# Working out the recurrence's gates in two halves: inside the first stage and inside attention

## The reference

```python
ig = (x @ Wi + bi).transpose(0, 2, 1)[..., None]      # x = [q, k, v]
fg = (x @ Wf + bf).transpose(0, 2, 1)[..., None]
log_f = jax.nn.log_sigmoid(fg)
log_f_cum = ... jnp.cumsum(log_f, axis=2)
log_D = tril(log_f_cum - log_f_cum^T) + ig^T
D = jnp.exp(log_D - max(log_D))
C = (qh @ kh^T) / sqrt(dh) * D
h = C / (max(|C.sum|, exp(-max_log_D)) + EPS) @ vh
```

## Time and profile before

| | us |
|---|---|
| median of 3 runs | 794.55 (789.97 to 797.62) |
| profiled execution | 790.37 |
| its span | 788.6 |
| first stages | 0 to 75.1 |
| gates' stage with its two ends | 75.1 to 104.5 |
| attention | 104.5 to about 314.5 |
| mixture | to 788.6 |

### The profile page before, as it was taken

How to read it: one execution, slowest core, us unless ns; L and a number is a source line. 1 busy time by engine, 2 the same in 40 slices (tenths; PEclk the granted TensorE clock), 3 DMA queues, 4 the chain that set the end, 5 groups by cost and what they waited for, 6 DMA issues and landing times.

```text
span 788.6 us, 20116 instructions
## 1 busy us (share of the span) xinstructions
PE 685.6 (87%) x7407; PEld 597.4 (76%) x7408; DVE 506.3 (64%) x992; ACT 409.3 (52%) x848; POOL 391.4 (50%) x594
## 2 busy tenths in 40 slices
PE   0785069999999886789999999999999999999994
PEld 0553057777777765678889998999999999999993
DVE  4762846777777787966338787533557666676750
ACT  0766246676666665544454232223556666666662
POOL 2111347888878875632111534132246675757654
PEclk9999579999999999999999999999999999999998
DMA  7982363544545721286761313243678787988854
GB/s 247 297 293 69 138 208 110 182 136 152 157 140 181 236 83 54 84 306 240 265 206 54 108 54 107 55 98 105 190 225 225 233 234 244 232 258 219 254 142 57
DMA packets 90726, 135.66 MB, mean 172 GB/s; under 512 B 16720, under 2 KB 44112, under 8 KB 90672
## 3 DMA queue, kind: packets, MB, share of 16 engines
q1 hardware_dynamic: 74128, 107.41, 41.7%
q0 software_dynamic: 7168, 17.04, 11.0%
q10 hardware_dynamic: 9376, 10.49, 4.2%
HBM read 92.32 MB, written 34.21 MB: 160 GB/s over the span
## 4 chain that ended last, share of the span: by engine, by line
PE 65%; DVE 7%; ACT 5%; DMA 4%; issue 2%; POOL 2%; SPq 0%; POOLq 0%; ACTq 0%; DVEq 0%
PE psH L1229 30%; PE psY L1249 15%; PE psO L702 4%; PE psQ L660 4%; PE ring L645 3%; PE ring L670 2%; ACT dec L744 2%; PE ring L676 2%; PE psT L1209 2%; DMA xT<-over13l 1%; DMA out<-ystage,sidx 1%; ACT state L757 1%; DMA amr<-am 1%; PE psR L1276 1%; DVE xl L1478 1%
## 5 line engine op out<-in xcount | busy, mean ns | idle before, releaser
L1229 PE MATMUL psH<-xh,w13h 128*128 128x256 f32 (+1 forms) x768 | 220.5, 287 | 2.8 <-issue 2.8
L1229 PE MATMUL psH<-xh,w13l 128*128 128x256 f32 (+1 forms) x768 | 215.2, 280 | 0.0
L1229 PE MATMUL psH<-xl,w13h 128*128 128x256 f32 (+1 forms) x768 | 214.9, 280 | 0.0
L1721 POOL TENSOR_TENSOR hl<-sg,hh 128x256 fp32r<-128x256 f32 (+1 forms) x96 | 79.4, 833 | 178.2 <-ACT hh L1352 177.7
L1229 PEld LDWEIGHTS psH<-xh,w13h 128*128 128x128 f32 (+1 forms) x768 | 137.8, 179 | 10.9 <-issue 10.0
L1229 PEld LDWEIGHTS psH<-xl,w13h 128*128 128x128 f32 (+1 forms) x768 | 138.0, 180 | 0.8
L1229 PEld LDWEIGHTS psH<-xh,w13l 128*128 128x128 f32 (+1 forms) x768 | 137.8, 179 | 0.0
L1347 ACT ACTIVATE sg<-psH 128x256 f32<-128x256 f32 (+1 forms) x96 | 36.4, 379 | 126.5 <-PE psH L1229 125.8
L1484 DVE TENSOR_TENSOR sg<-sg,psH 128x256 f32<-128x256 f32 (+1 forms) x96 | 39.9, 416 | 94.2 <-ACT sg L1347 94.2
L744 ACT ACTIVATE dec<-ring 128x512 f32<-128x512 f32 x128 | 74.0, 592 | 26.9 <-PE ring L648 26.2
L821 DVE SCALAR_TENSOR_TENSOR dec<-psQ,dec 128x512 f32<-128x512 f32 x128 | 79.3, 680 | 6.9 <-PE psQ L660 6.2
(11 more groups left out here) (224 smaller groups left out, 1397.5 us busy)
## 6 DMA issues: line engine op xcount, KB each, us to landing
raw<-w13T SPq DMA_DIRECT2D x64, 352.0 KB, 4.4
gcT<-ctxT ACTq DMA_DIRECT2D x8, 1024.0 KB, 5.8
kT<-ctxT SPq DMA_DIRECT2D x16, 512.0 KB, 5.6
ctxs<-ctx SPq DMA_DIRECT2D x16, 512.0 KB, 3.7
xn<-xnorm SPq DMA_DIRECT2D x16, 512.0 KB, 4.0
out<-xres SPq DMA_DIRECT2D x16, 512.0 KB, 4.8
raw<-w2T SPq DMA_DIRECT2D x16, 512.0 KB
qst<-qT_all SPq DMA_DIRECT2D x14, 512.0 KB, 6.4
```

The costliest lines, as they stand in the source:

```text
L1229: last = nc.tensor.matmul(psH[m][0:n, v, :], w[wp][:, c, col:col + n], x[xp][:, c, :], start=(c == 0 and k == 0), stop=(c == DC - 1 and k ...
L1721: nc.gpsimd.tensor_tensor(hs[u.p][1][0:n, m, :], sg[0:n, m, :], hs[u.p][0][0:n, m, :].bitcast(F32), ALU.subtract).then_inc(hl_ready, 1)
```

## The change

`gate_stage` is gone. What it did stands in four generators, one for each engine (`gates_vector`, `gates_scalar`, `gates_tensor`, `gates_saved` for SP), each working on one half of 256 columns; the code around it calls `next(gates)` where a piece shall run. Half 0 runs in the first stage (now `front_stage`), half 1 in attention.

- In the first stage the loops are written out. The gate rows of batches 0 to 7 are stored straight to `half.head` in SBUF, those of 8 to 15 to DRAM as before. VectorE does bias and absolute value ahead of measuring pair 7, `log1p_exp` between the norms of pairs 6 and 7, the rest behind. For pair 7 VectorE, not ScalarE, copies the queries from PSUM, in its `drain`. ScalarE does Exp and Ln at the end of step 5, the three exponentials and part 0 ahead of `keep(7)`, parts 1 and 2 behind; the subtractions are VectorE's. GpSimd builds the masks in steps 2 and 3. SP loads batch 0's keys and context between `store(5)` and `store(6)`; `store(7)` stands between the saves of part 1 and part 2; when all is saved it loads tile 0's decay rows, then the masks of the second buffers in three DMAs.
- The buffers of half 0 lie where `aml[1]` and `amr[1]` lie, those of half 1 on the first two batches of `qT_all` (the queries of batches 2 and 3).
- In attention tiles 0 to 14 are written out, then a loop of 3 x 4. VectorE has a piece at the end of tiles 6 (bias, absolute value), 7 (`log1p_exp`), 8 (F, am), 9 (M, -M, m), 10 (first subtraction), 11 (first `tmE` copy) and inside the take in tiles 11 (second subtraction), 12 and 13 (`tmE` copies). ScalarE has Exp and Ln in tile 7, three exponentials and part 0 in tile 10, parts 1 and 2 in tiles 11 and 12. TensorE has one transpose ahead of `back` in tiles 11, 12 and 13, all three into the same columns of `psO`. SP loads `head` in batch 3 and saves in batch 6; batch 8's decay load waits for the saves.
- The table load at attention's start is gone; tanh and the load of the exponentials' table are in step 3 of the first stage.

The diff, cut to its core (the removed stage is the one quoted above):

```diff
-                    sp.wait_ge(kept, 2 * p + k + 1)
+                    b = 2 * p + k
+                    sp.wait_ge(kept, b + 1)
                     for w in range(2):
-                        sp.dma_start(d.gt[w, bass.ds(2 * p + k, 1)].rearrange("b h t -> (b h) t"),
-                                     gst[k][w * NH:(w + 1) * NH, :]).then_inc(stored[k], 16)
+                        to = half.head[b * NH:(b + 1) * NH, w, :] if b < HB else d.gt[w, b]
+                        sp.dma_start(to, gst[k][w * NH:(w + 1) * NH, :]).then_inc(stored[k], 16)
...
-            for p in range(PAIRS - 4, PAIRS):
+            for p in range(4):
+                refill(p + 2, p % 2)
                 store(p)
+            for p in (4, 5):
+                store(p)
+            sp.dma_start(g.kT0[:, :, :], d.ctxT[0].rearrange("(c p) t -> p c t", p=P)).then_inc(g.kT_in[0], 16)
+            sp.dma_start(g.ctx0[:, :, :], d.ctx[0].rearrange("(c p) d -> p c d", p=P)).then_inc(g.ctx_in[0], 16)
+            store(6)
+            for n, _ in enumerate(gates_saved(sp, gt, half, 0, d)):
+                if n == 1:
+                    store(7)
+            sp.wait_ge(gt.saved, 16 * 4)
+            sp.wait_ge(gt.ex_turned, 3)
+            load_decay(sp, g, d, 0, 0, masks=(masks_ready, 2))
+            for rows, lo, hi in ((g.aml, 0, 3), (g.aml, 6, P), (g.amr, 3, P)):
+                sp.dma_start(rows[1][lo:hi, :, :], rows[0][lo:hi, :, :]).then_inc(g.masks_kept, 16)
             for k in range(2):
...
-            run(dve, step, lambda i, r: None, ch, 2 * 3)
+            gates = gates_vector(nc, g, gt, half, 0, ch, ((stored[0], 32 * 4), (stored[1], 32 * 4)), turned_to)
+            def step(p):
+                if p + 1 < PAIRS:
+                    if p + 1 == PAIRS - 1:
+                        next(gates)
+                    measure(p + 1)
+                norm(p)
+                if p == PAIRS - 2:
+                    next(gates)
+            def drain(p):
+                next(gates)
+                next(gates)
+                for k in range(2):
+                    n = 2 * p + k
+                    dve.wait_ge(xt_ready, n + 1)
+                    nc.vector.tensor_copy(g.qT_all[:, (n - 2) * DC:(n - 1) * DC, :], psT[k][:, :, :])
+                dve.wait_ge(tanh_ready, 1)
+                nc.vector.tensor_scalar(g.coef[:, :], g.coef[:, :], g.tanh[:, 0:1], None, ALU.mult)
+                for _ in gates:
+                    pass
+            measure(0)
+            run(step, drain)
         @block.gpsimd
         def _(pool):
...
+            gates = gates_scalar(nc, act, gt, half, 0)
...
+                if p == 3:
+                    act.wait_ge(later_in, 16 * LATER)
+                    nc.scalar.activation(g.tanh[:, :], g.branch[:, :], ACT.Tanh).then_inc(tanh_ready, 1)
+                    nc.scalar.preload_act_table_set("natural_log_exp_and_others")
+                if p == 5:
+                    next(gates)
+            def drain(p):
+                next(gates)
+                keep(p)
+                for _ in gates:
+                    pass
+            run(step, drain)
...
+def gates_vector(nc, g, gt, h, k, c, arrived, turned_to):
+    dve = c.eng
+    nc.vector.memset(h.ones, 1.0)
+    for sem, count in arrived:
+        dve.wait_ge(sem, count)
+    c.link(nc.vector.tensor_scalar(h.f, h.head[:, 1, :], g.bias[:, 1:2], None, ALU.add))
+    nc.vector.scalar_tensor_tensor(out=h.poly, in0=h.f, scalar=-1.0, in1=h.f, op0=ALU.mult,
+                                   op1=ALU.max).then_inc(gt.abs_ready, 1)
+    yield
+    dve.wait_ge(gt.e_ready, 2 * k + 1)
+    log1p_exp(nc, c, h.e, h.lu, h.poly, h.mask, (gt.e_ready, 2 * k + 2))
+    yield
+    c.link(nc.vector.scalar_tensor_tensor(out=h.f, in0=h.f, scalar=0.0, in1=h.lu, op0=ALU.min, op1=ALU.subtract))
+    c.link(nc.vector.tensor_tensor_scan(h.F, h.ones, h.f, 0.0, ALU.mult, ALU.add))
+    c.link(nc.vector.scalar_tensor_tensor(out=h.am[:, 0, :], in0=h.head[:, 0, :], scalar=g.bias[:, 0:1],
+                                          in1=h.F, op0=ALU.add, op1=ALU.subtract))
+    yield
+    c.link(nc.vector.tensor_tensor_scan(h.M, h.am[:, 0, :], h.am[:, 0, :], -3.0e38, ALU.max, ALU.max))
+    nc.vector.tensor_scalar(h.am[:, 1, :], h.M, -1.0, None, ALU.mult)
+    nc.vector.tensor_tensor(h.m, h.F, h.M, ALU.add).then_inc(gt.exps_go, 1)
+    yield
+    for q in range(2):
+        dve.wait_ge(gt.part_made, 3 * k + q + 1)
+        nc.vector.tensor_tensor(h.rest, (h.am, h.rest)[q], h.parts[q], ALU.subtract).then_inc(gt.rest_ready, 1)
+        yield
+    for n in range(3):
+        dve.wait_ge(gt.ex_turned, 3 * k + n + 1)
+        nc.vector.tensor_copy(g.tmE[:, n, k * P:(k + 1) * P], turned_to[n]).then_inc(gt.tm_taken, 1)
+        yield
+def gates_scalar(nc, act, gt, h, k):
+    act.wait_ge(gt.abs_ready, k + 1)
+    nc.scalar.activation(h.e, h.poly, ACT.Exp, scale=-1.0).then_inc(gt.e_ready, 1)
+    act.wait_ge(gt.e_ready, 2 * k + 1)
+    nc.scalar.activation(h.lu, h.e, ACT.Ln, bias=1.0).then_inc(gt.e_ready, 1)
+    yield
+    act.wait_ge(gt.exps_go, k + 1)
+    nc.scalar.activation(h.ex[:, 0, :], h.am[:, 0, 0:P], ACT.Exp, bias=h.am[:, 1, P - 1:P])
+    nc.scalar.activation(h.ex[:, 1, :], h.am[:, 1, P:S], ACT.Exp, bias=h.M[:, P - 1:P])
+    nc.scalar.activation(h.ex[:, 2:4, :].rearrange("p a t -> p (a t)"), h.m, ACT.Exp, scale=-1.0).then_inc(gt.exps, 1)
+    nc.scalar.activation(h.parts[0], h.am, ACT.Copy).then_inc(gt.part_made, 1)
+    yield
+    for q in range(1, 3):
+        act.wait_ge(gt.rest_ready, 2 * k + q)
+        nc.scalar.activation(h.parts[q], h.rest, ACT.Copy).then_inc(gt.part_made, 1)
+        yield
+def gates_tensor(nc, g, pe, gt, h, k, turned_to):
+    pe.wait_ge(gt.exps, k + 1)
+    for n, q in enumerate((0, 2, 3)):
+        if n > 0 and turned_to[n] is turned_to[n - 1]:
+            pe.wait_ge(gt.tm_taken, 3 * k + n)
+        nc.tensor.transpose(turned_to[n], h.ex[:, q, :], g.ident[:, :]).then_inc(gt.ex_turned, 1)
+        yield
+def gates_saved(sp, gt, h, k, d):
+    rows = slice(k * P, (k + 1) * P)
+    sp.wait_ge(gt.exps, k + 1)
+    sp.dma_start(d.em.rearrange("b h t -> (b h) t")[rows], h.ex[:, 1, :]).then_inc(gt.saved, 16)
+    for q in range(3):
+        sp.wait_ge(gt.part_made, 3 * k + q + 1)
+        sp.dma_start(d.am[:, q].rearrange("w b h t -> (b h) w t")[rows], h.parts[q]).then_inc(gt.saved, 16)
+        yield
+def load_decay(sp, g, d, b, c, masks):
+    sp.wait_ge(*masks)
+    sp.dma_start(g.aml[c][3:6, :, :], d.am[0][:, bass.ds(b, 1), :, c * P:(c + 1) * P].rearrange(
+        "q b h t -> q (b h) t")).then_inc(g.am_in[c], 16)
+    sp.dma_start(g.amr[c][0:3, :, :], d.am[1][:, bass.ds(b, 1), :, c * P:(c + 1) * P].rearrange(
+        "q b h t -> q (b h) t")).then_inc(g.am_in[c], 16)
...
-        R0, RPL, LOOPS = 3, 4, 6
+        R0, RPL, LOOPS = 15, 4, 3
...
+        GATES_ACT, GATES_DVE = (14, 20, 22, 24), (13, 15, 17, 19, 21, 23)
+        GATES_PE = (10, 11, 12)
+        turned_to = [psO[:, 0, 264:264 + P]] * 3
...
+                if b == HB:
+                    sp.wait_ge(gt.saved, 16 * 8)
+                load_decay(sp, g, d, b, 0, masks)
                 sp.wait_ge(qsc_ready, b)
                 load_em(b)
...
+                if b == 3:
+                    for u in range(2):
+                        sp.wait_ge(q_in[u], 16 * 2)
+                    sp.dma_start(half.head, d.gt.rearrange("w b h t -> (b h) w t")[P:2 * P]).then_inc(gt.head_in, 16)
                 sp.wait_ge(filled, decays_done(2 * b - 1))
-                load_decay(b, 1)
+                load_decay(sp, g, d, b, 1, masks)
+                if b == 6:
+                    for _ in gates_saved(sp, gt, half, 1, d):
+                        pass
                 if b == B - 3:
                     sp.wait_ge(q_in[0], 16 * (B // 2 - 2))
...
+                    next(gates)
                 for gg in range(4):
...
+                if r < R0 and 2 * r in GATES_ACT:
+                    next(gates)
...
-            nc.scalar.preload_act_table_set("natural_log_exp_and_others")
+            gates = gates_scalar(nc, act, gt, half, 1)
...
+                if r in GATES_PE:
+                    next(gates)
...
             def step(i, r, is_last):
                 for k in range(4):
                     weigh(i, r, k, decay_use(i, r, k))
+                if r < R0 and 2 * r in GATES_DVE:
+                    next(gates)
                 if r >= 1:
                     take(i, r - 1)
                 if r >= 2:
                     residual(i, r - 2)
+                if r < R0 and 2 * r + 1 in GATES_DVE:
+                    next(gates)
+            gates = gates_vector(nc, g, gt, half, 1, c_, ((gt.head_in, 16),), turned_to)
...
+                        pool.wait_ge(gt.tm_taken, 6)
                     keys(i, r + 1)
                     lift_values(i, r + 1, 0)
```

## The result

The changed kernel takes 803.06 us (median of 4 runs, 801.68 to 807.0) where the kernel before, on the same chip, takes 796.09 (4 runs): a ratio of 1.013, 95% interval 1.0092 to 1.0169. The forecast was 781.4. The profiled execution took 801.95, its span 799.9 where that of before is 788.6: 11.3 us longer.

The account below looks back on a forecast made before the run. A 29.4 us hole ahead of attention was taken as the bound: span 788.6 - 20.1 (front) + 7.0 (attention) = 775.5; against the median, 794.55 - 13.1 = 781.4 us, range 773 to 790.

Parts of the forecast that it names:

- The hole can be taken out: The 29.4 us gates' stage ahead of attention: what is taken from it comes off the end, unless attention gives it back.
- The store's wait: First stage, before measuring pair 7: VectorE waits for a 2.5 us gate-row store, shifting the rest by 1.5 us, bounds 0 and 4.
- The first decay at 83.5: Start of attention: the first decay matmul comes at 83.5 where it was 104.59, a gain of 21.1 us.
- The barrier falls under that load: Between first stage and attention: the block's barrier is hidden under tile 0's 2.3 us decay load.
- Tile 1's masks: Attention's tile 1: decay rows behind the mask copies, landing 2.5 to 5.6 us after issue, stall it 0 to 2.2, taken +1.0.
- The clock: Attention's start: TensorE again idles about 6 us beforehand, so nothing is given back for the slow first tile.
- Attention: Gates' work moved into attention's tiles costs +7.0 us: 5.0 of work, 2.0 of VectorE-GpSimd collisions; bounds 4 and 17.
- collisions dear: Rival: VectorE-GpSimd port collisions make attention cost +12 to +17 us, giving 786.5 to 791.5; chance 0.15.
- SP in batch 6: SP stands until tile 12 for part 2; tile 14's keys and decay load behind it aren't due earlier, costing nothing.
- The signs: Wrong if the first decay is after 90, or attention up to tile 14 loses under 3 or over 12 us.
- same: Outcome within one per cent of the median: half the poor-front and dear-collision rivals plus the hole that stays; chance 0.16.
- slower: Outcome slower than before: a rival at 805, twenty VectorE operations each behind a whole GpSimd one, had 0.04; outcome's chance 0.05.

Follow-up runs that it names:

- e3: The changed kernel with VectorE's bias and absolute value behind pair 6's norm, log1p behind pair 7's, ScalarE's Exp and Ln in step 6; 798.7 us, ratio 1.0067.
- e5: e11 with the mask copies issued behind the block's barrier and TensorE's wait for the weights moved to the first back; 782.71 us, ratio 0.9873.
- e11: The changed kernel with the edits of e1, e2 and e3 together, ScalarE's Exp and Ln a little earlier; 780.88 us, ratio 0.9855.
- e4: The kernel before with fourteen serial copies of mask rows to a spare buffer, to price partition counts; 128 partitions took 2.92 us, 122 took 12.73.
- e1: The changed kernel with its two large mask copies cut at row 16, into 112 and 10 or 13 partitions; 792.55 us, ratio 0.9978.
- e8: e5 with tile 0's keys first, mask copies on two queues, tile 1's decay load ahead of em, and TensorE waiting for the masks; 782.51 us, ratio 0.985.
- e12: e8 with VectorE's second-half gate pieces mostly between weighs and take, other engines' pieces following a tile later; 780.0 us, ratio 0.9853.
- e2: The changed kernel with SP's save of the second half's part 2 moved behind batch 7's keys and first decay load; 796.97 us, ratio 1.0027.
- e9: e8 with 40 more unread transposes in TensorE's wait ahead of attention; 783.92 us, ratio 0.9868.

## Why the prediction was wrong, by its steps

**The hole can be taken out.** Right. With the three places mended the same change gives 0.9855, some 11.5 us, where the forecast had 13.1. The hole's wait for pair 7's own chain was costed well: from the end of `sums(7)` to the last save landed the forecast has 8.1 us (73.1 to 81.2), after has 7.2 (78.3 to 85.45).

**The store's wait (+1.5, bounds 0 and 4).** Wrong, and outside the bounds: 5.0. The 2.5 us is a median of 32 stores over the whole stage, half of them with little beside them; the trace of before has 4.6 as the median of those issued from 40 to 52 us and 1.5 of those behind 56. This one is issued at 55.35, some 0.9 us later than I had it, behind a load of 1 MB that ScalarE issued at 54.63, and takes 4.88. The upper bound was also added up wrongly: with 5.6 us for the store it is 1.5 + 3.1 = 4.6, not 4. That the large load is the cause was not tested by an edit, but the traces of all the changed kernels agree: the stores of this pair issued ahead of that load landed in 2.2 to 4.0 us, those behind it in 4.8 to 5.3, all of them into SBUF. In before, where they go to DRAM, the last one took 3.5, so a part may be the new destination's. What followed from it wasn't in the sum either: TensorE stood idle 7.11 us ahead of pair 7's transposes and did them at 1.2 GHz in 3.68 us, not 1.97, so `sums(7)` ended at 78.3, 5.2 late. e3 shows the same place mended: 3.4 us.

**The first decay at 83.5.** Right as a time of the data: with the barrier out of the way it is 82.9 in e5. "The barrier falls under that load" was wrong, since SP issues 3 mask copies ahead of it (8.26 us of "PEq L142" at 89.58). In e11 it makes the first decay 2.4 late and leaves the queries 1.07 waiting for GpSimd's set-up. Moving it out of the way gains nothing, though, as the copies then hold tile 1: e11 with that barrier is as early at the take of tile 0 as e5 without it.

**Tile 1's masks (+1.0, 0 to 2.2).** This is the step that failed: 12.67 us. I took the 5.6 us of `aml<-aml` as the price of a mask copy. That copy has all 128 partitions; the diff's have 122 and 125, and their count decides (12.73 and 7.85 against 2.92 in e4). Both numbers stood in the diff, and nothing in the trace of before showed such a count. The Trainium skill (DMA: Bandwidth & Descriptors, Why a DMA increments its semaphore by 16 and not by 1) has the rule: by it 122 partitions go out over 2 engines of 16. e1, which changes only the counts, gives 11.8 us back at the take of tile 0. Mended they hold it no more where they are issued ahead of the barrier (e1, e11), and by 3 us where they are issued behind it (e5, e8).

**The clock ("I give back nothing").** Too kind by a little. In before the half clock ended at 107.9, 3.3 us behind the first decay; in e5 it lasted until 97, 14 us behind it. Of the forecast front of -20.1, e11 reaches -15.8 and e12 -18.3. In e11 the rest is a first decay that comes 2.4 late (85.92 against 83.5) and 2.8 more than before from there to the take, 1.07 of them GpSimd's set-up and some 1.8 the half clock, where the forecast had 1.0 for tile 1's rows.

**Attention (+7.0, of it 5.0 of work and 2.0 of collisions).** Near in sum, 6.3 to tile 11, and in part by luck. Two collisions are plain, 0.9 and 0.6 beyond the length of their operations, where I had three of 0.8. They are part of the undisturbed 5.1, so that some 3.6 are left for the work, where I had 5.0. Another 1.2 came with a half clock (156 to 159 us), behind TensorE's wait of 1.61 us for the weighs, which I had not thought of and which made good a part of what was too high. Rival "collisions dear" (12 to 17) is refuted by every kernel (at most 8.9, e1). The lock itself is as the Trainium skill (SBUF — State Buffer, Who interferes with whom) has it, whoever is second waits; but in after only two of VectorE's added operations met it (1.32 and 1.09) and two of GpSimd's (1.52 and 1.49 for 1.04).

**SP in batch 6 ("Nothing").** Wrong: 4.2 us. I argued that the decay load of tile 14 isn't due before tile 12's part 2; it isn't, but behind the save stand first 1 MB of keys and queries, then the load, whose own landing took 4 us. e2 shows the 4.2 gone. The step named what was queued behind the wait and then did not add up their times.

**The signs.** Neither sign that was to show me wrong came: the first decay was at 89.58, not after 90, and attention lost 10.6 to tile 14, not over 12. The wait of tile 1 had been given as up to 2 us and was 12.67, and no limit was set for it. (In the chances, "same" adds up to 0.17 and "slower" to 0.04, not 0.16 and 0.05.)

**The sum.** Forecast less measured, at the take of tile 0: 19.9 us (-20.1 against -0.2), of which e1 shows 11.8, e3 3.4, e11 both, 15.6; the 4 that are left are e11's late first decay, GpSimd's set-up and the clock. Attention -0.7, tile 14 +4.2, behind it +0.6. Together 24.0; the spans differ by 11.3 and the forecast by -13.1, which is 24.4.

## What to carry to other kernels

Before a DMA is costed from another, compare the counts of its slowest dimension, not only the bytes: cut 122 rows into 10 and 112. When a hole in front of a stage is closed, the end of the gain is not the first instruction of that stage but the first one that waits for what had been hidden in the hole, so cost the second tile too, and give it a sign of its own. And where a queue stands at a wait, add up everything behind it until the load that matters has landed.

## What the runs showed of the hardware

- A copy of 122 partitions of 4 KB took 12.73 us, one of 128 2.92, one of 112 3.60; two odd ones beside each other held their queue 18 us.
- A VectorE operation of 8 columns took 1.07 us beside GpSimd's of 1.04 that began with it, where its neighbours took 0.17.
- A store of 16 KB took 4.8 to 5.3 us when a load of 1 MB had been issued just ahead of it on the other queue, and 2.2 to 4.0 when it was issued ahead of the load (stores of batches 6 and 7, all changed kernels).
- TensorE fell to 1.2 GHz around short waits too: after has a half clock from 64 to 71 (a wait of 7.11 us until 66.38), 156 to 159 (1.61 us until 154.80) and 197 to 200 (3.22 us until 197.38), which before doesn't have; a wait of 2.16 us until 170.60 brought none. In e9 the 40 transposes began at 77.46 at half clock, and the clock was back at 2.4 GHz at 83.2, before they ended at 84.80.
